# A fused four-layer kernel: the second query projection moved behind the turned maxima in turns 3 to 7, and a copy and a score product moved ahead of weight passes in the first turn

## What is computed

```python
x = x + tanh(g_xattn[0]) * causal_attention(ln(x), ctx, ctx)          # 16 heads of 32
x = x + tanh(g_ffn[0])   * ternary_ffn(ln(x), w_gate_up, w_proj)      # weights by groups of 64
x = x + tanh(g_xattn[1]) * cross_attention(ln(x), ctx, q_w, k_img_w, v_img_w, o_w, ...)
x = x + tanh(g_ffn[1])   * quantised_ffn(ln(x), w_norm, w_gv, w_out)  # 8-bit inputs, ternary weights
```

## Time and profile before

| | |
|---|---|
| median of 3 runs | 1124.33 us (1123.89 to 1126.89) |
| the profiled execution, own time | 1122.95 us |
| its span, first to last instruction | 1121.0 us |
| its mean granted TensorE clock | 0.997 of full speed |
| TensorE busy | 1093.6 us, 98% of the span |
| VectorE, ScalarE, GpSimd busy | 74%, 51%, 10% |

### The profile page before, as it was taken

One profiled execution on the slowest core, in us unless ns is written; L12 is line 12 of the kernel. 1 busy time (PEld: TensorE's weight loads), 2 busy tenths in 40 slices (PEclk: granted clock), 3 DMA queues, 4 the chain that ended last, 5 costly groups with the idle time before them and its releaser, 6 DMA issues.

```text
span 1121.0 us, 25577 instructions
## 1 busy us (share of the span) xinstructions
PE 1093.6 (98%) x10386; PEld 661.7 (59%) x10386; DVE 832.5 (74%) x1437; ACT 567.4 (51%) x918; POOL 117.3 (10%) x212
## 2 busy tenths in 40 slices
PE   8899999999999999999999999999999999999998
PEld 3455555556777777777777655555554545454543
DVE  4888888778676657566565667986868787778795
ACT  4767666765433323333333352464554547372654
POOL 1101100110000000000001122120202020201010
PEclk9999999999999999999999999999999999999999
DMA  9655555433212011021010201101010101000001
GB/s 361 205 188 182 187 190 174 147 107 124 67 39 66 20 39 38 20 76 38 20 58 20 85 1 39 39 2 57 1 58 1 58 1 39 1 11 10 11 10 38
DMA packets 29267, 79.24 MB, mean 71 GB/s; under 512 B 3040, under 2 KB 3296, under 8 KB 28896
## 3 DMA queue, kind: packets, MB, share of 16 engines
q1 hardware_dynamic: 29152, 77.61, 21.2%
HBM read 65.02 MB, written 12.58 MB: 69 GB/s over the span
## 4 chain that ended last, share of the span: by engine, by line
PE 91%; DVE 4%; ACT 2%; issue 2%; DMA 1%; SPq 0%; POOL 0%; ACTq 0%; DVEq 0%; POOLq 0%
PE bank L699 10%; PE bank L593 10%; PE bank L594 10%; PE bank L681 10%; PE bank L554 9%; PE bank L804 9%; PE bank L434 5%; PE bank L834 5%; PE bank L792 5%; PE bank L754 3%; PE bank L773 3%; PE bank L486 2%; PE bank L459 2%; PE bank L507 2%; PE bank L519 2%
## 5 line engine op out<-in xcount | busy, mean ns | idle before, releaser
L593 PE MATMUL bank<-ARENA,W 128*128 128x256 f16 x1024 | 227.3, 273 | 0.7 <-issue 0.7
L594 PE MATMUL bank<-ARENA,W 128*128 128x256 f16 x1024 | 227.3, 273 | 0.0
L1012 ACT ACTIVATE ARENA<-bank 128x512 f32<-128x512 f32 (+3 forms) x143 | 93.0, 687 | 71.7 <-PE bank L434 31.8
L681 PE MATMUL bank<-W,ARENA 128*128 128x512 bf16 x512 | 120.8, 379 | 0.0
L804 PE MATMUL bank<-W,ARENA 128*128 128x512 bf16 x512 | 119.3, 383 | 0.4 <-DVE W L1753 0.4
L554 PE MATMUL bank<-ARENA 128*128 128x512 f32 x256 | 117.8, 602 | 0.7 <-DMA ARENA<-in_wkv 0.7
L699 PE MATMUL bank<-ARENA 128*128 128x512 f32 x256 | 116.9, 599 | 0.0
L593 PEld LDWEIGHTS bank<-ARENA,W 128*128 128x128 bf16 x1024 | 100.2, 98 | 19.1 <-issue 1.3
L594 PEld LDWEIGHTS bank<-ARENA,W 128*128 128x128 bf16 x1024 | 100.2, 98 | 18.0
L1012 ACT ACTIVATE ARENA<-ARENA 128x512 f16<-128x512 f32 x64 | 40.3, 630 | 133.2 <-DVE ARENA L1607 129.5
L2031 POOL TENSOR_TENSOR ARENA<-ARENA 128x2 f32<-128x2 f32 (+1 forms) x72 | 49.6, 689 | 507.1 <-DVE ARENA L1387 267.4
(11 more groups left out here) (181 smaller groups left out, 1801.9 us busy)
## 6 DMA issues: line engine op xcount, KB each, us to landing
W<-in_w SPq DMA_DIRECT2D x48, 512.0 KB, 4.3
ARENA<-in_w SPq DMA_DIRECT2D x24, 512.0 KB, 3.6
kv_store<-ARENA SPq DMA_DIRECT2D x32, 256.0 KB, 4.3
W<-kv_store SPq DMA_DIRECT2D x15, 512.0 KB, 4.0
ARENA<-in_ctxT SPq DMA_DIRECT2D x8, 512.0 KB, 3.8
X<-in_x SPq DMA_DIRECT2D x8, 512.0 KB, 6.1
ARENA<-in_ctx SPq DMA_DIRECT2D x8, 512.0 KB, 6.1
out<-X SPq DMA_DIRECT2D x16, 256.0 KB, 2.0
```

Source lines behind the costliest of these rows:

```text
L593: pe.matmul(bank[:, i * S:(i + 1) * S], W0[:, at:at + P], xt_half(b, 0)[:, k, :], start=(k == 0), stop=False)
L594: mm = pe.matmul(bank[:, i * S:(i + 1) * S], W0[:, at:at + P], xt_half(b, 1)[:, k, :], start=False, stop=(k == KD - 1))
L681: mm = pe.matmul(banks[6 + t], hx(q, what)[:, i * S + t * P:i * S + (t + 1) * P], W0[:, UP_AT + m * D:UP_AT + (m + 1) * D], start=(m == 0 ...
L1012: return act.activation(to, src, ACT.Copy)
```

## The change

In turns 3 to 7 TensorE's second half has another order: the score product g = 3 comes right after value-gate product 4, products 5 to 7 follow it, then the turned maxima, and only then the second query projection. Behind the first probability pass `d_turn_u(d, 0)` takes the place of `c_turn_q(f)`, which goes behind the second pass. ScalarE and VectorE follow: `c_square_q(f, 1)` comes behind the switch to the table of Exp, the two copies of `d_turn_u` come ahead of those of `c_turn_q`, and VectorE splits `d_value_gate` into product and reduction, so that products 5 and 6 follow each other. The bank `ut0.1` moves from bank 7 to bank 5, between `g7` and `tq1`. In the first turn of stage a ScalarE copies the projected keys and takes the exponentials of group 1 ahead of `a_abs_sum` 0 and 1, and VectorE reduces the scores of group 2 ahead of `a_distance(b, 1)`, and those of group 3 with their maxima ahead of `a_ternary(b, 1)`.

```diff
-            places.turn(turn, ("g0 v1 g3 pq0 v6 v7 ut0.0 y0 xt0", "v0 po1 v3 g4 v5 g7 tq1 w1 w2 w3", "po0 g2 kt0 v4 pq1 w0 qt1 ut1.1 y1",
-                               "g1 v2 kt1 g5 g6 mt tq0 ut0.1 qt0 ut1.0 xt1"))
+            places.turn(turn, ("g0 v1 g3 pq0 v6 v7 ut0.0 y0 xt0", "v0 po1 v3 g4 v5 g7 ut0.1 tq1 w1 w2 w3", "po0 g2 kt0 v4 pq1 w0 qt1 ut1.1 y1",
+                               "g1 v2 kt1 g5 g6 mt tq0 qt0 ut1.0 xt1"))
...
                 c_project_q(f, 0)
                 d_value_gate(d, 4)
+                c_scores(b, 3)
                 d_value_gate(d, 5)
-                c_scores(b, 3)
+                d_value_gate(d, 6)
+                d_value_gate(d, 7)
+                c_max_turn(b)
                 c_project_q(f, 1)
-                d_value_gate(d, 6)
-                c_max_turn(b)
-                d_value_gate(d, 7)
                 c_probs(b, 0)
+                d_turn_u(d, 0)
+                c_probs(b, 1)
                 c_turn_q(f)
-                c_probs(b, 1)
                 c_weigh(b, 0)
-                d_turn_u(d, 0)
                 c_probs(b, 2)
...
                 a_group_mean(b, 2)
-                if not end:
-                    a_abs_sum(b, 0)
-                a_abs_sum(b, 1)
+                if end:
+                    a_abs_sum(b, 1)
                 if front:
                     a_projected(f, 0)
                 else:
                     a_projected(b, 3)
                 a_probs(b, 1)
+                if not end:
+                    a_abs_sum(b, 0)
+                    a_abs_sum(b, 1)
                 a_abs_sum(b, 2)
...
                 d_gate(d, 5)
-                c_square_q(f, 1)
                 d_gate(d, 6)
                 d_gate(d, 7)
                 warm(ACT.Exp)
+                c_square_q(f, 1)
                 c_probs(b, 0)
+                both(d_turn_u, d, 0)
+                c_probs(b, 1)
                 c_turn_q(f)
-                c_probs(b, 1)
-                both(d_turn_u, d, 0)
                 c_probs(b, 2)
...
                 if back:
-                    a_distance(b, 1)
                     if turn == 1:
                         a_scores(b, 2)
-                    a_ternary(b, 1)
+                    a_distance(b, 1)
                     if turn > 1:
+                        a_ternary(b, 1)
                         a_scores(b, 2)
...
                     a_max_rows(b, 1)
+                    if turn == 1:
+                        a_ternary(b, 1)
...
                 d_value_gate(d, 4)
-                d_value_gate(d, 5)
                 c_norm_q(f, 0)
                 c_scores(b, 3)
                 c_max_parts(b)
-                d_value_gate(d, 6)
+                d_gated(d, 5)
+                d_gated(d, 6)
+                d_largest(d, 5)
                 c_max_rows(b)
                 d_integers16(d, 0)
+                d_value_gate(d, 7)
                 c_norm_q(f, 1)
-                d_value_gate(d, 7)
                 d_scale_u(d, 1)
```

5 lines of the change are left out of this document (added).

## The result

The changed kernel takes 1127.22 us (median of 22 runs, 1123.51 to 1130.11) beside 1123.58 us for the kernel before (22 runs). The ratio is 1.0028, 95% interval 1.0018 to 1.0037: slower by 2.0 to 4.2 us. I had forecast 1125.5 us, in a range of 1121.5 to 1129.5, and no measurable change as the likeliest case. The direction is right. The size is not: I had added 1.15 us to the median before, a ratio of 1.0010, and the measured 0.28% is nearly three times that. It still lies within the 0.3% either way to which I gave most of the chance, but with 22 runs of each kernel the interval reaches only 0.1% to either side, and no change at all lies outside it.

A forecast was written before the change was run, and what follows sets the result against it. TensorE was taken as the bound, busy 1093.6 of 1121.0 us. Five later turns at +1.85 and the first turn at -0.7 us gave +1.15 on the median 1124.33: 1125.5 us, range 1121.5 to 1129.5.

The forecast's parts named there:

- (b): Products 5 to 7 in a row: g6 waits for g5's bank until its silu ends, 0.15 us a turn (0 to 0.2).
- (c): g7 waits for v5's bank, as v5's multiplication stands behind VectorE's reduction of group 3: 0.15 us a turn.
- (a): Score product g = 3, now behind one value-gate product, waits for VectorE's reduction of group 2: 0.15 us a turn (0 to 0.4).
- (d): At the turned maxima the wait goes, since g6 is long read out: -0.15 us a turn; VectorE's copy stays hidden.
- (f): Between the probability passes u's turning replaces the queries': the 1.06 us loss stays; behind the second pass 0.1 us more or nothing.
- (g): tq1 takes the bank of ut0.1, which ScalarE copies out after both exponentials: a wait of 0.05 to 0.1 us a turn.
- (e): The second projection's square, root and scaling finish before the queries' turning behind the second pass: under 3 of 4.75 us, cost 0.
- The loss at the second pass: Second probability pass waits for the first's exponentials, 1.06 us a turn, forecast to stay; rival that it goes: chance 0.08.
- GpSimd's hold on VectorE: GpSimd's bias additions to x might block VectorE in turns 3 to 7, growing (c) by up to 1 us a turn; chance 0.03.
- The first turn: In stage a's first turn the third probability pass starts at about 45.5 instead of 46.22: 0.7 us gained.
- starts at about 33.65: First turn: with the copy out of bank 1 moved ahead, the score product starts then instead of 35.71, 2.05 us gained.
- The clock rival: A clock fall to 1.2 GHz after the first turn's second idle stretch costs some 1.7 us: 1127.2 us in all; chance 0.12.

The follow-up runs named there:

- gates: Kernel before with only the new order of products, turned maxima and second query projection in turns 3 to 7, turnings and banks as before: ratio 1.0031.
- gap_first_mt: gap_first with the turned maxima of turns 3 to 7 in the bank of value product 5 and g7 in that of g6: ratio 0.9935 to before.
- first: Kernel before with only the change's half in the first turn of stage a, the last stages as before: ratio 1.0011.
- first_sum0: Kernel before with the change's first-turn half, but absolute sum 0 kept ahead of the copy of the projection: ratio 0.9974.
- gap_first: gap and first_sum0 joined: both turnings between the first two probability passes, and absolute sum 0 ahead in the first turn: ratio 0.9945 to before.
- swap: Kernel before with only the two turnings exchanged in turns 3 to 7, with the banks this gives: ratio 1.0012.
- gap: Kernel before with both turnings, queries then u, between the first and second probability passes in turns 3 to 7, one bank moved: ratio 0.9976.

## Why the prediction came out as it did

- **Turns 3 to 7: +0.40 a turn forecast, +0.58 measured.** The mechanism was right, and two terms were too small. (b) and (c) together were 0.30 in the sum and cost 0.45: removed by other banks alone. The rows put 0.25 us ahead of g6, where I had 0.15 and at most 0.2, and 0.11 us ahead of g7, where I had 0.15. The last 0.10 us stands at v7, where I had written "done about when g7 ends: 0": v7 waits for the multiplication of product 6. (a) was 0.15 and is 0.19 (the reduction ends at 795.39, the score product starts at 795.64); in turn 3 it falls away, as I had it, and that turn costs 0.48 us for the forecast's 0.25. (d) was -0.15 and is -0.21, of which the wait of the earlier trace rows is 0.13. (f) and (g) were 0.1 and are 0.14.
- **(e)** held: the norm is ready before the turning of the queries behind the second pass. Gates shows its price when it isn't covered: 1.35 us of waiting, 0.24 us of it in the turn.
- **The loss at the second pass** stayed: 4.75 us from the first pass to the end of the second, as (f) said, and it was there to be had by another edit.
- **GpSimd's hold on VectorE** did not come: the reduction of scores took 2.35 us, 0.96 us of it beside a GpSimd addition. The Trainium skill's page "SBUF — State Buffer", section "Who interferes with whom", says that on trn2 a tensor_reduce never contends with GpSimd, and that an instruction with at most one SBUF input doesn't either, outside the 2-port modes. The trace now agrees for the reduction too. In the first turn I had counted a hold of 0.96 us on a tensor_tensor. It didn't come there either, since the addition (34.34 to 35.62) now stood beside a reduction that took its 1.22 us; the reduction of group 2 ended at 37.48 where I had 38.4. Nothing followed from it, since ScalarE set the third pass.
- **The first turn: -0.7 forecast, +0.9 to +1.0 measured.** This is the part that came out the other way. Two steps failed. The first is that the score product "starts at about 33.65": I read what stood ahead of the copy on ScalarE and not what the copy writes to, a staging buffer that a store must leave first. It started at 34.55. That cost nothing in the end, since the chain through ScalarE set the third pass, as I had worked out: absolute sum 2 at 40.73 (40.5 forecast), released by its load, the third pass at 45.65 (45.5), released by ScalarE, 0.57 us earlier than before. Two errors cancelled in it: sum 0 started 0.6 us later than I had it (35.57 for 34.95), and from there to sum 2 it took 5.16 us in place of 5.53. The step that turned the sign is the granted clock, which I left out of the sum: the projection behind the pass lost 1.6 us, and the second turn came 1.04 us later than before, as that rival said (+1.0). I gave it 0.12; it came in all five traces of this first turn, behind idle stretches of 2.5 to 3.1 us, where I had reckoned with 1.7 us. Its 1.7 us were also not what the text beside them says: the third pass and the projection, 1.1 and 3.7 us, doubled would be 4.8 us more. The half clock held for only a part of them (5.30 us for the projection).
- **The time.** Turns 3 to 7 cost 2.8 us where I had 1.85, and the first turn 0.9 to 1.0 us where I had -0.7: 3.7 to 3.8 us for the forecast's 1.15, within the measured 2.0 to 4.2. The clock rival had this first turn and gave 1127.2 us, the measured median. It was the least likely but one in my list, and that it came to the very figure is luck: it did so with last stages that were 0.9 us too cheap and a start that was 0.7 us too high (1124.33 of three runs, 1123.58 of 22).

## What to carry to other kernels

When products are moved into one row, count the distance in products between two users of the same bank, against the time from a product's start until its reader has ended plus the signal; such a wait can show as no idle time of TensorE, only as a group that is longer than its like and in the rows of the weight loads. When an edit is meant to remove a wait for a bank, look who takes that bank now: in gap_first_mt the wait only moved to the next user. Before an instruction is moved forward, read every semaphore that it waits on at its new time, the buffer that it writes to included. And where a profile shows a fixed time from one pass to the next that some other engine sets, fill it with work from behind it: exchanging what stands in it gained nothing here.

## What the runs showed of the hardware

- The granted clock fell to half (1.2 GHz of 2.4) shortly after an idle stretch of TensorE of 2.52 us in the changed kernel, 2.93 us in first and 2.47 us in gates, and in the first two a projection of eight matmuls took 5.30 and 4.48 us for 3.70. Where the same stretch was 0.34 us (first_sum0) or 0.64 us (gap_first) it did not fall. The fall from 36.4 to 39.6 is less regular: it came in the changed kernel behind 1.52 us of idle time and in gap_first_mt behind 1.63 us, and not in first_sum0 behind 1.42 us nor in first behind 1.19 us; and it stayed out in gates behind 2.35 us, where before had it behind the same 2.35 us. The length of one idle stretch alone doesn't tell: in turn 8 the stretch of 1.28 us behind the first probability pass is followed by a fall in the changed kernel and by none in swap.
- The mean granted clock of a whole execution, 0.991 to 1.000, explains most of the spread of 6 to 7 us between executions of one kernel: 0.94 us for 0.001. In the traces it is lost in the first 60 us and in turn 8 alone. I had taken that spread for noise; taking it out gave intervals of half a microsecond.
- From the start of the first probability pass to the end of the second it took 4.75 us with three contents of the gap, in before, the changed kernel and gap alike, since the second pass waits for ScalarE's exponentials.
- A bank was taken again 0.11 us after the silu or the multiplication that read it had ended (changed kernel, products 6 and 7).
